# A four-layer graph network on one Trainium2 core: the second hop and the first node stage joined slot by slot, three addition tables cleared in the setup, list work spread between other slots

## The chip, the cores and the metric

One core of a Trainium2 chip. The metric is the device time of the whole program in microseconds (us), lower is better. One launch computes everything.

## The reference, cut to what matters

50000 nodes with 256 features (f32), 50000 edges sorted by destination. Four layers, each `x = layernorm(x + layer(x))`:

```python
# layer 0: two hops of a normalised graph convolution
for _ in range(2):
    msg = segment_sum(norm[:, None] * h[src], dst, N)
    h = 0.5 * msg + 0.5 * x
h = relu(h) @ W.T + b
# layers 1, 2: attention over incoming edges (8 heads), with edge features
attn = softmax over the edges of one dst of leaky_relu(scores)
out  = segment_sum(h_src * attn, dst) + bias
# layer 3: filtered messages, summed by SOURCE node, then two dense layers and a batch norm
msg = x[dst] * (silu(rbf @ Wf1 + bf1) @ Wf2 + bf2)
agg = segment_sum(msg, src, N)
h = silu(agg @ Wu1 + bu1) @ Wu2 + bu2; out = x + batchnorm(h)
```

## The kernel before, in words

Rows (edges or nodes) are padded to 50176 = 128 partitions x C = 392 columns; partition p holds the rows p*392 to p*392+391. Nodes are kept in "edge order": a node's row stands where its first or last edge stands, and nodes without an edge stand at free places. Lists made in the setup say which node's input (`input_i`), which turn of rows (`turn_i`) and which final row (`node_i`) belongs to each place. A stage runs over slots of G = 2 or 4 columns, with a ring of NS buffers per tile. Each engine has its own program; `hold` waits on the semaphore of an earlier slot or stage. The number beside a stage in `unrolled`/`written` is its lag in slots. A stage ends, and so does every `nc.Block()`, only when all five engines, SyncE (SP) among them, have come to its end. SP and ScalarE issue plain DMAs, GpSimd (POOL) the indirect ones: gathers by a list and adding scatters.

The stages, in order, with the first line of each one's main gather where it has one:

- `setup` (L155 to L640). Block 1: 28 loads and 5 small fills from SP (L211, L214), then one DMA of all of x into the table XT (L215, 50176 rows of 1 KB), while VectorE (DVE) prepares flags. Block 2: a histogram of degrees and in-counts, one column at a time (L344, L345 DVE, L354 POOL, L363 ScalarE, L372 and L375 TensorE), with a ring of 4. Block 3: short arithmetic. Block 4, nearly all DVE: `locate` and `compress` (L498 to L524) for two lists, FREE and EMPTY, a join over TensorE, `expand` (L538 to L556) for EMPTY, then SP writes four numbers per node into XT (`XT<-degs`, L637, 50176 runs of 32 bytes); meanwhile DVE runs `expand` for FREE and makes `input_i`; two gathers of border rows `brow` (L630, L631) wait for the write and feed `turn_i`.
- `hop_edges(0)` (gather L681 from XT) and `hop_edges(1)` (gather L681 from S0): slots of 2 columns, ring of 7. Hop 1 per slot: 2 gathers of S0 rows, a load of XE rows (L660), DVE mixes them (L733) and adds along the destination's run (L742), SP stores the sums to the table S1 (L669). A small block at the end carries the last run of each partition over to the place `start_e`.
- `layer_nodes(0)` (gather L879 from x by `input_i`): slots of 2 columns, ring of 4. Load of S1 rows (`st`, L863), 2 gathers of x, DVE mixes (`yt`, L925), adds the bias (L894), adds the product (`z`, L946), and runs the layer norm's statistics; ScalarE rectifies and copies; TensorE transposes, multiplies by W0, transposes, multiplies by the next layer's table weights; ScalarE stores X1 and T1.
- `attention_edges(1)`, `layer_nodes(1)`, `attention_edges(2)`, `layer_nodes(2)`: the attention stages have slots of 4 columns and a ring of 4. SP's order there is, per step: edge attributes of slot t (L1095), store of S of slot t-2 (L1101), then `empty`: a 512 KB DMA of zeros into the addition table A[layer-1] (L1105).
- `filter_edges`: slots of 2 columns; the first column of a slot is added into A[0], the second into A[1] by an adding scatter (L1386); each waits until the one before it on the same table has landed. DVE's compare (L1467) and ScalarE's copy wait for the adds of four slots earlier.
- `update_nodes`: loads A[0] and A[1], adds them (DVE), two dense layers (TensorE), stores. `finish_nodes`: batch norm, layer norm, gather L1635, output.

Of the kernel before, what the change touches and what calls it, by code (L numbers as in the profile page):

```python
# [18 lines left out]
P = 128  # L19
D = 256  # L20
H = 8
# [61 lines left out]
def build(nc, N, x, src, dst, dst_prev, dst_next, ew, rbfT, attr3T, attr64T, w0T, b0, w1T, w1, a1, encW, bias1,  # L83
# [33 lines left out]
    def dram(name, rows, width):  # L117
        return nc.dram_tensor(name, (rows, width), F32).ap()
# [8 lines left out]
    A = [dram("A0", NP + P, D), dram("A1", NP + P, D)]  # L127
    HT = nc.dram_tensor("HT", (P, K, C * P), F32).ap()

    with ExitStack() as keep:  # L130
# [5 lines left out]
        isfirst, notfirst, islast, notlast, follows = [sb(n, [P, C]) for n in ("isfirst", "notfirst", "islast", "notlast", "follows")]  # L136
        head_i, tail_i, start_e = sb("head_i", [P, 1], I32), sb("tail_i", [P, 1], I32), sb("start_e", [P, 1], I32)
# [15 lines left out]
        stats = sb("stats", [P, K, C // 2, 6])  # L153


        def setup():
            with ExitStack() as ctx:
# [3 lines left out]
                def sem(name):  # L161
                    return semaphore(name)

                dst_f, prev_i, next_i, near = tmp("dst_f", [P, C]), tmp("prev_i", [P, C], I32), tmp("next_i", [P, C], I32), tmp("near", [P, C])
# [7 lines left out]
                rowid, free, empty, frees, empties = [tmp(n, [P, C]) for n in ("rowid", "free", "empty", "frees", "empties")]  # L172
                firsts, lasts = tmp("firsts", [P, C]), tmp("lasts", [P, C])
                below = tmp("below", [P, 2])
                deg, ok, dinv, sq = tmp("deg", [P, C]), tmp("ok", [P, C]), tmp("dinv", [P, C]), tmp("sq", [P, C])
# [17 lines left out]
                loaded, zeroed, iotas, prep, tr, folds, filled, widened, placed = [sem(n) for n in (  # L193
                    "loaded", "zeroed", "iotas", "prep", "tr", "folds", "filled", "widened", "placed")]
# [12 lines left out]
                with nc.Block() as block:  # L207
                    @block.sync
                    def _(e):
                        for to, frm in loads:  # L210
                            e.dma_start(to, frm).then_inc(loaded, 16)  # L211
                        e.wait_ge(zeroed, 1)
                        for to, frm in fills:
                            e.dma_start(to, frm).then_inc(filled, 16)  # L214
                        e.dma_start(XT[:, 0:D], x.rearrange("p c d -> (p c) d")).then_inc(widened, 16)  # L215

                    @block.gpsimd
                    def _(e):
                        e.memset(zero[:], 0.0).then_inc(zeroed, 1)
                        e.memset(degs[:], 0.0).then_inc(iotas, 1)  # L220
# [20 lines left out]
                    def _(e):  # L241
# [58 lines left out]

                        for node, at, to_i, to, off in ((dst_f, col, part_i, part, over),):
# [11 lines left out]
                    def _(e):  # L313
# [12 lines left out]
                        mm.then_inc(folds, 1)  # L326

                with nc.Block() as block:  # L330
                    NS = 4
                    R = C // NS
                    hots, taken, masks, maskcs = [stage_of(n, NS) for n in ("hots", "taken", "masks", "maskcs")]
# [6 lines left out]
                    def _(e):  # L340
                        def one_hot(i, s):
                            c = bass.ds(i * NS + s, 1)
# [38 lines left out]
                with nc.Block() as block:  # L381

                    clamped, rooted, based, carried = sem("clamped"), sem("rooted"), sem("based"), sem("carried")
                    DEG, NUMBER, LEAD, ROW = 3, 9, 18, 27

                    @block.vector
                    def _(e):
# [17 lines left out]
                        link(e.tensor_tensor_scan(frees[:], unit[:], notfirst[:], 0.0, ALU.mult, ALU.add))  # L405
# [6 lines left out]
                        link(e.tensor_copy(below[:], psB[:, 3:5]))  # L412
# [36 lines left out]
                        link(e.tensor_scalar(m_half[:], m_half[:], 0.5, None, ALU.mult))  # L449

                    @block.tensor
                    def _(e):
                        e.wait_ge(clamped, NUMBER)
                        e.matmul(psB[:, 0:1], before[:], number[:, C - 1:C], start=True, stop=True)
                        e.matmul(psB[:, 3:4], before[:], empties[:, C - 1:C], start=True, stop=True)
                        e.matmul(psB[:, 4:5], before[:], frees[:, C - 1:C], start=True, stop=True).then_inc(based, 1)
# [12 lines left out]
                with nc.Block() as block:  # L469
                    banks.close()  # L470
                    BITS, CODE = 10, 512.0
                    rem, rev, bit, near2 = tmp("rem", [P, C]), tmp("rev", [P, C]), tmp("bit", [P, C]), tmp("near2", [P, P])
                    rowsC, pos, pcol1 = tmp("rowsC", [P, P]), tmp("pos", [P, W]), tmp("pcol1", [P, 1])
                    pk0, pk1, ck0 = [[tmp(f"{n}{j}", [P, 1]) for j in range(2)] for n in ("pk0", "pk1", "ck0")]
                    oh = [[tmp(f"oh{j}{h}", [P, P]) for h in range(2)] for j in range(2)]
                    ohT = [[tmp(f"ohT{j}{h}", [P, P]) for h in range(2)] for j in range(2)]
                    listed, owner = [tmp(f"listed{j}", [P, W]) for j in range(2)], tmp("owner", [P, W])
                    codes, other, moved = [tmp(n, [P, 2, W]) for n in ("codes", "other", "moved")]
                    joint, there, shift = tmp("joint", [P, 2, C]), tmp("there", [P, W]), tmp("lshift", [P, W])
                    ids, r1, r2 = tmp("ids", [P, C]), tmp("r1", [P, C]), tmp("r2", [P, C])  # L480
                    brow = tmp("brow", [P, 2, XW])
                    bank = lambda n: ctx.enter_context(psum(n, [P, 512], F32))
                    psO, psJ, psL = bank("psO"), [bank(f"psJ{j}") for j in range(2)], [[bank(f"psL{j}{h}") for h in range(2)] for j in range(2)]
                    counted, located, turned, ready, assembled, copied, fetched, taken, tabled, placed, bounded = [sem(n) for n in (
                        "counted", "located", "oturned", "ready", "assembled", "jcopied", "lfetched", "ltaken", "rtabled", "placed", "bounded")]
                    EMPTY, FREE = 0, 1

                    @block.vector
                    def _(e):
# [6 lines left out]

                        def locate(j):
                            link(e.tensor_scalar(near2[:], rowsC[:], below[:, j:j + 1], None, ALU.is_le))  # L498
                            link(e.tensor_reduce(pk1[j][:], near2[:], AX, ALU.add))
                            link(e.tensor_scalar(pk0[j][:], pk1[j][:], -1.0, None, ALU.add))  # L500
# [1255 lines left out]
```

## Time and profile before

| | us |
|---|---|
| median of 3 runs | 7849.68 (7843.85 to 7850.1) |
| the profiled execution | 7853.95 |
| its span (first to last instruction) | 7852.0 |
| DVE / PE / POOL / ACT busy in the span | 6030.9 / 4153.3 / 3600.6 / 3581.2 |

PE is TensorE, ACT ScalarE. The profile shows one execution. The rows further down give times from the start of the span. "Busy" leaves out semaphore, register and DMA-issuing instructions; rows with SPq show how long SP was occupied with issuing a DMA.

### The profile page before, as it was taken

What the parts mean: (1) busy time and instruction counts of PE and PEld (TensorE: products, weight loads), DVE (VectorE), ACT (ScalarE), POOL (GpSimd) and SP (SyncE); (2) the same over time, 40 slices, a digit from 0 to 9 for tenths busy, and PEclk for the clock granted to TensorE, in tenths of its full rate; (3) what the DMA queues carried; (4) which work ended last, traced back from release to release, by engine and by line L of the source; (5) the groups of instructions that cost most, each with busy time, mean ns of one, the idle gap of its engine ahead of it and who ended that gap; (6) DMA issues with size and microseconds to landing.
All of it is one profiled execution on the core that took longest, in us unless ns stands there. A gap on an engine that the chain in (4) does not pass through costs nothing. (4 is left out here: it accounts for less than half of the span.)

```text
span 7852.0 us, 84021 instructions
## 1 busy us (share of the span) xinstructions
PE 4153.3 (53%) x18168; PEld 3161.6 (40%) x18168; DVE 6030.9 (77%) x18094; ACT 3581.2 (46%) x9619; POOL 3600.6 (46%) x3559
## 2 busy tenths in 40 slices
PE   7910000039999333335886222000498998999644
PEld 4500000038888222223554222000266666888522
DVE  7896657767776899998998777899888885554676
ACT  4505750038888333334775000234444443444688
POOL 7806767764443333334555555000266662000477
PEclk9955555569999555557998555555699999999755
DMA  9028989978787566667998888677677776666799
GB/s 285 1 6 236 313 295 298 299 252 243 243 243 227 201 220 220 217 219 249 341 342 276 263 264 264 223 251 252 174 114 115 114 113 147 203 203 204 242 316 304
DMA packets 1120799, 1765.08 MB, mean 225 GB/s; under 512 B 227356, under 2 KB 586372, under 8 KB 1120170
## 3 DMA queue, kind: packets, MB, share of 16 engines
q1 hardware_dynamic: 683786, 1019.20, 40.7%
q0 software_dynamic: 188768, 422.51, 21.9%
q10 hardware_dynamic: 247744, 318.00, 11.7%
q8 instruction: 155, 2.54, 0.1%
q14 instruction: 346, 2.83, 0.1%
HBM read 969.63 MB, written 840.95 MB: 231 GB/s over the span
## 5 line engine op out<-in xcount | busy, mean ns | idle before, releaser
L1125 POOL DMA_INDIRECT rows<-T,index_i x784 | 759.4, 969 | 884.2 <-DVE sums L1267 698.5
L817 ACT ACTIVATE xo<-z,shift,rsd 128x256 f32<-128x256 f32 x1568 | 849.8, 593 | 0.4 <-issue 0.2
L1635 POOL DMA_INDIRECT xt<-X,node_i x392 | 370.8, 946 | 908.4 <-POOLq L1702 784.6
L1386 POOL DMA_INDIRECT A<-comb,ai x392 | 617.6, 1575 | 340.4 <-DMA A<-comb,ai 227.1
L1142 PE MATMUL psE<-encs,attr 4*128 4x256 f32 x784 | 369.7, 649 | 635.5 <-DMA attr<-in_attr3T 633.3
L879 POOL DMA_INDIRECT xt<-in_x,input_i x392 | 375.2, 957 | 470.6 <-DVE xb L894 394.2
L766 PE MATMUL psC<-sums,chainT 128*128 128x256 f32 x4 | 2.4, 700 | 1100.6 <-PEq L655 1100.6
L1401 PE MATMUL psH<-rbf,wf1s 20*128 20x256 f32 x784 | 228.4, 411 | 644.7 <-DMA rbf<-in_rbfT 644.7
L789 DVE BATCH_NORM_STATS2 row_stats<-z 128x6 f32<-128x256 f32 x1568 | 564.5, 402 | 0.1
L1142 PEld LDWEIGHTS psE<-encs,attr 4*128 4x128 f32 x784 | 243.9, 326 | 760.9 <-DMA attr<-in_attr3T 702.2
L801 ACT ACTIVATE sd<-mean_var,epsc 128x2 f32<-128x2 f32 x784 | 237.9, 303 | 584.8 <-DVE mean_var L796 583.0
L879 POOL DMA_INDIRECT xt<-X,turn_i x392 | 370.4, 945 | 251.8 <-DVE xb L894 185.0
L1044 PE MATMUL psV<-w2s,xT 128*128 128x272 f32 x1568 | 407.2, 403 | 114.6 <-ACT tt L980 114.6
L681 POOL DMA_INDIRECT rows<-S,index_i x392 | 396.8, 1012 | 122.7 <-issue 99.8
L766 PEld LDWEIGHTS psC<-sums,chainT 128*128 128x128 f32 x4 | 1.0, 310 | 1102.4 <-issue 1102.4
L1142 PE MATMUL psE<-fes,attr 64*128 64x8 f32 x784 | 183.3, 360 | 493.2 <-DMA attr<-in_attr64T 485.2
L681 POOL DMA_INDIRECT rows<-XT,src_i x392 | 379.1, 967 | 141.7 <-issue 100.9
L959 ACT ACTIVATE yt<-yt,m_half 128x256 f32<-128x256 f32 x392 | 183.2, 532 | 559.9 <-DVE yt L925 559.9
L1589 DVE COPY aT<-psA 128x512 f32<-128x512 f32 x196 | 135.5, 691 | 379.1 <-PE psA L1540 379.1
L1401 PEld LDWEIGHTS psH<-rbf,wf1s 20*128 20x128 f32 x784 | 133.8, 189 | 723.9 <-DMA rbf<-in_rbfT 644.8
L742 DVE SCALAR_TENSOR_TENSOR sums<-sums,follows,rows 128x256 f32<-128x256 f32 x784 | 381.1, 486 | 21.3 <-issue 0.3
L1159 ACT ACTIVATE rowsd<-rowsd,isfirst 128x280 f32<-128x280 f32 x392 | 174.9, 516 | 486.0 <-DMA rowsd<-T 486.0
(358 smaller groups left out, 14805.5 us busy)
## 6 DMA issues: line engine op xcount, KB each, us to landing
X<-xo ACTq DMA_DIRECT2D x588, 256.0 KB, 3.6
S<-sums SPq DMA_DIRECT2D x196, 544.0 KB, 2.8
st<-S SPq DMA_DIRECT2D x392, 272.0 KB, 4.2
S<-sums SPq DMA_DIRECT2D x392, 256.0 KB, 4.0
A<-zero SPq DMA_DIRECT2D x196, 512.0 KB
T<-tt ACTq DMA_DIRECT2D x196, 280.0 KB
rowsd<-T SPq DMA_DIRECT2D x98, 560.0 KB
T<-tt ACTq DMA_DIRECT2D x196, 272.0 KB
```

The source lines that it names most:

```text
L681: e.indirect_dma_start(rows[s][:, k, :], None, table, bass.IndirectOffsetOnAxis(ap=at_i[:, c:c + 1], axis=0))\
L742: ins = e.scalar_tensor_tensor(sums[s][:, k, :], last, follows[:, bass.ds(C - (i * NS + s + 1) * G + k, 1)], rows[s][:, k, 0:D], ALU.mult, ...
L789: ins = e.bn_stats(row_stats[s][:, k, :], z[s][:, k, :])
L801: e.activation(sd[s][:, :, 0], mean_var[s][:, :, 1], ACT.Sqrt, bias=epsc[:]).then_inc(signal(rooted, s), 1)
L817: ins = e.activation(y[s][:, k, :], z[s][:, k, :], ACT.Identity, bias=shift[s][:, k, :], scale=rsd[s][:, k, :])
L879: e.indirect_dma_start(xt[s][:, k, :], None, xin, bass.IndirectOffsetOnAxis(ap=at_i[:, c:c + 1], axis=0))\
L1044: mm = e.matmul(psV[k][:, 0:DW], xT[s][:, k, m * P:(m + 1) * P], weights[:, m, :], start=m == 0, stop=m == K - 1)
L1125: e.indirect_dma_start(rows[s][:, k, :], None, table, bass.IndirectOffsetOnAxis(ap=at_i[:, c:c + 1], axis=0))\
L1142: mm = e.matmul(psE[s % 2][:, k * EW:(k + 1) * EW], attr[s][:, k, :], weights[:], start=True, stop=True)
L1386: e.indirect_dma_start(A[k], bass.IndirectOffsetOnAxis(ap=ai[s][:, k, :], axis=0), comb[s][:, k, :], None, compute_op=ALU.add).then_inc(si ...
L1401: mm = e.matmul(psH[s % 2][:, m * G * P:(m + 1) * G * P], wf1s[:, m * P:(m + 1) * P], rbf[s][:].rearrange("p g q -> p (g q)"), start=True, ...
L1635: e.indirect_dma_start(xt[s][:, k, :], None, X3, bass.IndirectOffsetOnAxis(ap=node_i[:, c:c + 1], axis=0))\
```

## The change

1. `hop_edges(1)` and `layer_nodes(0)` become one stage, `hop_nodes`, of 196 slots of 2 columns. The sums go from the hop's DVE add straight to the node part's mix, one slot later, from on-chip memory; S1 is still stored but no longer loaded. A longer block at the end redoes the one row per partition that needs the carry: through both products and the norm, into X1 and T1.
2. `A` has three tables. All are cleared in the setup's block 1 by SP, 294 DMAs of 512 KB; `empty` is gone from the attention stages. The adds of `filter_edges` go round the three tables; `update_nodes` loads and adds a third.
3. List work: the FREE list's `locate`, `distance`, bit and shift steps run one piece per 17 columns inside the histogram; its `shift_right` steps and the making of `input_i` and `turn_i` run one piece per 8 slots in hop 0, where the two `brow` gathers now stand ahead of the first gather. Three small reductions (`fix_sum`, `fix_half`, `fix_i`) are added to block 3.

```diff
+    A = [dram(f"A{t}", NP + P, D) for t in range(3)]
 ...setup, block 1, SP...
+                        e.wait_ge(zeroed, 2)
                         for to, frm in fills:
                             e.dma_start(to, frm).then_inc(filled, 16)
                         e.dma_start(XT[:, 0:D], x.rearrange("p c d -> (p c) d")).then_inc(widened, 16)
+                        for t in A:
+                            for c in range(0, C, QZ):      # QZ = 4
+                                e.dma_start(nodes(t)[:, c:c + QZ, :], wide_zero[:]...).then_inc(emptied, 16)
 ...histogram, DVE...
+                        def one_hot(i, s):
+                            if (i * NS + s) % EVERY == EVERY - 1:      # EVERY = 17
+                                list_free((i * NS + s) // EVERY)
 ...block 4, SP...
                         e.dma_start(nodes(XT)[:, :, D:XW], degs[:]).then_inc(placed, 16)
                         e.wait_ge(placed, 16)
+                        e.wait_ge(emptied, 16 * len(A) * (C // QZ))
 ...hop 0, DVE...
+        unrolled(R, NS, ... [(weigh, 0), (square, 0), (weight, 0), (add, 2), (list_rows, 0)])
 ...hop_nodes (new): POOL, DVE, PE...
+                        every([(gather, 0), (take, 0)])            # 2 gathers of S0, 2 of x
+                        every([(mix_hop, 0), (mix, MIX), (add_hop, 0), (add_bias, MIX), (add, ADD), (ln_invert, APPLY),
+                               (ln_stats, ADD), (ln_shift, APPLY), (ln_measure, ADD)])
+                        every([(turn_r, TURN), (multiply, PRODUCT), (turn_x, TURNX), (tabulate, TABLE)])
+                MIX, TURN, PRODUCT, ADD = 1, 2, 3, 4
+                APPLY, TURNX, TABLE = 5, 6, 7
 ...attention, SP...
-                        written(N, NS, ... [(stage, 0), (store, 2), (empty, 2)])
+                        written(N, NS, ... [(stage, 0), (store, 2)])
 ...filter, POOL...
+                                q = (i * NS + s) * G + k
+                                hold(e, *landed(q - len(A)))
+                                e.indirect_dma_start(A[q % len(A)], ..., compute_op=ALU.add).then_inc(added[q % len(A)], 16)
 ...update, DVE...
+                            e.tensor_tensor(more[s][:], more[s][:], third[s][:], ALU.add)...
```

In `hop_nodes` the rings of the gathers, loads and sums hold 7 slots, the others 4. `gather(t)` waits for the hop's add of slot t-7, `take(t)` (the gather of x) for the mix and bias of slot t-7.

## Rows read from the trace of the kernel before

**Rows 1.** Windows, one per stage; the heading is the first line.

```profile
core 0: us, PE busy (x) PEld busy (x) DVE busy (x) ACT busy (x) POOL busy (x), PEclk, DMA share, GB/s
628.00:1148.00 520.00, 1.19 (x2) 0.50 (x2) 305.43 (x1381) 363.38 (x980) 381.19 (x394) 0.50 0.91 301
1148.00:1680.00 532.00, 1.19 (x2) 0.50 (x2) 367.73 (x793) 0.00 (x0) 398.86 (x394) 0.50 0.88 291
1680.00:2565.00 885.00, 871.86 (x4696) 748.82 (x4696) 614.00 (x1964) 727.46 (x2151) 375.21 (x392) 0.99 0.78 238
...
3600.00:4265.00 665.00, 515.50 (x2369) 370.32 (x2368) 627.23 (x2369) 481.99 (x1570) 374.22 (x396) 0.97 0.98 323
4265.00:4950.00 685.00, 185.21 (x792) 175.76 (x792) 496.11 (x1386) 36.70 (x196) 373.95 (x391) 0.50 0.80 256
...
5595.00:6575.00 980.00, 860.97 (x3532) 602.72 (x3532) 791.65 (x2560) 437.97 (x1184) 618.52 (x393) 0.95 0.69 113
6575.00:7340.00 765.00, 763.97 (x3910) 673.05 (x3911) 379.91 (x779) 327.39 (x781) 0.00 (x0) 1.00 0.63 200
```

**Rows 2.** Timeline, one add in layer_nodes(0): start, us, engine, and idle time before it.

```profile
2100.87 0.69 DVE L946 TENSOR_TENSOR z<-psZ,xb 128x512 f32<-128x512 f32 x1 [1.31 <-issue]
```

**Rows 3.** Groups by line in hop 1: busy us, mean ns, idle before and releaser.

```profile
L681 POOL DMA_INDIRECT rows<-S,index_i x392 | 396.8, 1012 | 122.7 <-issue 99.8 <-DVE sums L742 19.5 <-PEq L655 3.4
L742 DVE SCALAR_TENSOR_TENSOR sums<-sums,follows,rows 128x256 f32<-128x256 f32 x392 | 190.2, 485 | 14.0
L733 DVE SCALAR_TENSOR_TENSOR rows<-rows,w_from,xe 128x256 f32<-128x256 f32 x392 | 173.5, 483 | 139.5 <-DMA rows<-S,index_i 132.0 <-issue 4.4 <-DVE sums L742 0.4
```

**Rows 4.** Timeline of the setup: SP's issues, the histogram's start, the last write, hop 0.

```profile
0.80 0.40 SPq L211 DMA_DIRECT2D src_i<-in_src  x1
...
14.12 0.43 SPq L211 DMA_DIRECT2D bts<-in_beta  x1
...
17.06 0.63 SPq L215 DMA_DIRECT2D XT<-in_x  x1
18.03 0.36 DVE L251 CAST src_f<-src_i 128x392 f32<-128x392 int32 x1 [18.03 <-DMA bts<-in_beta]
...
51.04 1.28 ACT L363 ACT_TABLE_LOAD   x1 [51.04 <-PEq L207]
...
563.46 0.61 SPq L637 DMA_DIRECT2D XT<-degs  x1
...
602.40 1.87 POOL L630 DMA_INDIRECT brow<-XT,dst_i  x1 [227.69 <-SPq L469]
...
628.74 0.94 POOL L681 DMA_INDIRECT rows<-XT,src_i  x1 [22.57 <-PEq L655]
```

**Rows 5.** Timeline of the setup's DVE: begin and end of the FREE list's compress.

```profile
415.23 0.57 DVE L507 TENSOR_TENSOR rem<-cols,frees 128x392 f32<-128x392 f32 x1
...
458.21 0.57 DVE L527 TENSOR_SCALAR owner<-listed 128x784 f32<-128x784 f32 x1
```

**Rows 6.** Windows: the copy of x beside the histogram; a store of S alone.

```profile
100.00:150.00 50.00, 50.00 (x184) 27.54 (x183) 43.08 (x123) 31.47 (x61) 48.27 (x62) 1.00 1.08 320
...
3001.40:3002.70 1.30, 0.00 (x0) 0.00 (x0) 1.19 (x4) 0.88 (x4) 0.99 (x2) 0.50 0.99 378
```

**Rows 7.** Attention 2: SP's issue of the attributes, and PE that waits for them.

```profile
4602.87 0.98 SPq L1095 DMA_DIRECT2D attr<-in_attr64T  x1
...
4607.91 1.87 PE L1142 MATMUL psE<-fes,attr 64*128 64x8 f32 x8 [5.09 <-DMA attr<-in_attr64T]
```

**Rows 8.** Waits in attention 2, 4300 to 4920 us: total, times, longest.

```profile
DVE dot L1237 <- PE psE L1142: 134.8, 85, 3.0
```

**Rows 9.** Waits in attention 1, 2600 to 3560 us.

```profile
DVE enc L1231 <- ACT psX L1165: 24.8, 60, 1.0
```

**Rows 10.** Waits in filter_edges, 5650 to 6500 us.

```profile
POOL A L1386 <- DMA A<-comb,ai: 209.9, 173, 2.1
DVE eq L1467 <- DMA A<-comb,ai: 89.0, 120, 3.0
```

More of the change, by code:

```diff
@@ L326, in _ @@
                         mm.then_inc(folds, 1)
+                        e.wait_ge(freed, 1)
+                        e.matmul(psB[:, 4:5], before[:], frees[:, C - 1:C], start=True, stop=True)
                 with nc.Block() as block:
@@ L574, in _ @@
                         expand(EMPTY, 1)
+                        for b in reversed(range(BITS)):
+                            shift_right(e, link, b)
+                        identify(e, link, ids)
                         link(e.tensor_tensor(ids[:], ids[:], empty[:], ALU.mult))
@@ L682, in gather @@
                                     .then_inc(signal(gathered, s), 16)
+                        if not hop:
+                            for j, c in enumerate((0, C - 1)):
+                                e.indirect_dma_start(brow[:, j, :], None, XT, bass.IndirectOffsetOnAxis(ap=dst_i[:, c:c + 1], axis=0)).then_inc(bounded, 16)
                         unrolled(R, NS, [(gather, 0)])
@@ L1444, in copy @@
                             hold(e, *done(joined, i, s))
-                            hold(e, *done(added[0], i, s, NS))
-                            hold(e, *done(added[1], i, s, NS))
+                            for k in range(G):
+                                hold(e, *landed((i * NS + s - NS) * G + k))
                             e.copy(comb[s][:].rearrange("p g d -> p (g d)"), psM[s % 2][:]).then_inc(signal(copied, s), 1)
@@ L1461, in compare @@
                             hold(e, *done(joined, i, s, NS))
-                            hold(e, *done(added[0], i, s, NS))
-                            hold(e, *done(added[1], i, s, NS))
+                            for k in range(G):
+                                hold(e, *landed((i * NS + s - NS) * G + k))
                             for k in range(G):
@@ L1583, in add @@
                             hold(e, *done(loaded, i, s))
+                            e.tensor_tensor(more[s][:], more[s][:], third[s][:], ALU.add).then_inc(signal(paired, s), 1)
+                            hold(e, *done(paired, i, s))
                             e.tensor_tensor(agg[s][:], agg[s][:], more[s][:], ALU.add).then_inc(signal(summed, s), 1)
```

502 lines of the change are left out of this document (398 added, 104 removed).

## The prediction

> **What bounds the kernel now.** I read the stage windows first [rows 1], then for each touched stage the groups, the waits and a stretch of the timeline. The windows show a sequence of stages with different limits. Hop 1 (532 us) runs no TensorE to speak of and is bound by POOL: its 392 gathers took 396.8 us and the gaps between them 122.7, together 519.5 of 532, or 1.325 us per gather [rows 3]; DVE waits 132 us for the gathers. Layer_nodes(0) (885 us) is bound by PE: busy 871.9 us at a granted clock of 0.99, the 2.4 GHz level; DVE idles 1.31 us before each add [rows 2]. So one stage leaves PE idle and the next leaves POOL (375 of 885 us) and DVE (614 of 885) half idle. The setup is one long DVE chain after the histogram, which starts at 51.0 us when every engine has left block 1 [rows 4]. Attention 2 waits for edge attributes: PE sat 5.09 us before a matmul for a DMA that SP had issued 5.04 us before [rows 7], and DVE waited for that PE 134.8 us [rows 8]. The filter stage waits for its own scatters to land [rows 10].
>
> All sums are made against the profiled execution: span 7852.0, time 7853.95, which is 4.3 us above the median 7849.68. Such a kernel's runs spread by under 0.1%, and 0.2% is about what can be told from no change.
>
> **The fused stage.** It removes the load of S1 and one stage boundary; each slot of 2 columns now has all the rest. Per slot:
> - POOL: 4 gathers. At hop 1's 1.325 us [rows 3]: 5.30. Layer_nodes(0)'s gathers were shorter, 375.2/392 = 0.957 us [rows 1], and with hop 1's gap of 0.31 they would give 5.08.
> - DVE: node part 614.0/196 = 3.13 [rows 1]; hop part 2 x 0.485 + 2 x 0.483 = 1.94 [rows 3]; sum 5.07. Its waits in both stages were for others, and go.
> - PE: 885/196 = 4.52 with the ends, unchanged work. It is no longer the bound.
> - DMA: 4 transfers of 262 KB (S0 rows, XE, S1 store, x rows), X1's 262 KB and T1's 287 KB: 1.60 MB. Layer_nodes(1) moved 323 GB/s at a share of 0.98 [rows 1], so 4.94 us.
> Three resources stand within 7% of each other. The rings of 7 slots give POOL and SP six slots of lead, so I take the longest, 5.30, and not a sum. The ends of the range are 5.07 (DVE alone) and 5.9: the DMA shares of the two stages added, 0.88 x 532/196 + 0.78 x 885/196 = 2.39 + 3.52 = 5.91, as if nothing else overlapped better.
> The stage: 196 x 5.30 = 1039. To it come the first gather's fill (8, an estimate from hop 0, whose first DVE work came 4 us after its first gather and here needs four), the drain of 8 slots (35, an estimate: seven more node slots at about 4.5), and the new end block, some 20 dependent steps with three DMA landings (25, an estimate at 0.5 us a step and 4 us a landing). About 1107 us for the 532 + 885 = 1417, which includes the boundary: **-310**. Range by the slot's two ends: -355 to -193.
>
> **The clock.** PE's share falls from 0.99 to about 4.45/5.3 = 0.84. Layer_nodes(1) held 0.97 with PE busy 515 of 665 us (77%) and the filter 0.95 with 88% [rows 1], so I cost it at nothing. If it fell to the 1.2 GHz level the PE slot would be about 8.9 us (below).
>
> **Clearing three tables in the setup.** 294 DMAs of 524 KB, 154.1 MB, issued by SP in block 1 behind the copy of x. Two prices.
> First, SP's issuing: from src_i to bts 28 loads took (14.12 - 0.80)/27 = 0.49 us each [rows 4]; 294 x 0.49 = 144 us. Block 2 can't start until SP is through, and SP reaches the first clear at 17.7. The copy of x was issued in 0.63 us although it moves 50176 rows, so its descriptors are made after SP has let go; how long the next issue waits is not shown. `XT<-degs`, as many runs, was wholly landed 38.9 us after its issue (563.46 to 602.40) [rows 4], so I take 39. Block 1 then ends at 17.7 + 39 + 144 = 201 instead of 51: **+150**.
> Second, the data. In order behind the copy (51.4 MB at 320 GB/s, to about 180 us [rows 6]), the clears take 154.1 MB at 378 GB/s, the rate of a store of S [rows 6], 408 us, and end near 590. At the copy's 320 they end at 662. The write of degs, at 680 below, comes behind both, so this costs nothing if SP need not wait for the data. Whether it must is what I am least sure of. SP ran ahead of its loads by several microseconds (the last, issued at 14.12, was followed by DVE's start on it at 18.03, with no issue stretched) [rows 4]; but that is some 2 MB, not 154.
> The Trainium skill, "Perfetto Trace Analysis", section "DMA Instruction — HWDGE (DVE, Sync)", says the descriptor generator is locked for one DMA until all its descriptors are made, and that a full buffer makes the DMA engines start before. By that rule SP's clears would advance no faster than the data, once the buffer is full; the 0.63 us row contradicts it for the issuing instruction itself and leaves it open for the next. It is the first rival below.
>
> **List work.** FREE's locate and compress leave block 4: 458.2 - 415.2 = 43 [rows 5] and about 3 of small steps. In the histogram DVE was busy 43.1 of 50 us [rows 6], so it has 0.138 x 326 = 45 us to spare for 46; pieces of 2.5 us meet a ring of 4 columns of 0.83 us, so I take 8 us of stalls. Bounds: 0 and 46. The three reductions add 4. `degs` is then ready at 563.5 + 150 + 8 + 4 - 46 = 680. The write's landing is next late: 39, to 719; FREE's expand before it is some 12 us and hidden, and the rest, the shifts, input_i and turn_i (about 50 us), moves to hop 0. There DVE is busy 305 of 520 us [rows 1] and a piece of 4 us meets a ring of 7 slots of 2.6 us: nothing, 50 if the cover failed. The two brow gathers, 1.9 us each [rows 4], now stand before hop 0's first. Hop 0's first gather: 719 + 1.5 + 3.7 = 724 against 628.7 [rows 4]: the setup costs **+95** in all (+50 if the copy holds up nobody, +210 if SP resumes only when the copy has ended near 180).
>
> **Attention 2 and 1.** Without the 512 KB of zeros the attribute DMA is issued half a microsecond earlier and lands behind 0.55 MB instead of 1.07. At 378 GB/s that is 1.4 us earlier [rows 6], 1.9 in all, against DVE's wait of 134.8/85 = 1.6 us per slot [rows 8]. **-130**; bounds 0 and -150. The next limit is DVE itself. Attention 1's DVE waited 24.8 us [rows 9] and was else busy: **-5**, bounds 0 and -25.
>
> **Filter.** With three tables a scatter waits for the third before it. POOL's 209.9 us and DVE's 89.0 us in 850 [rows 10] both end on landings. DVE gets back at most 89.0 x 980/850 = 103, then it is the bound (busy 792 of 980 plus gaps), PE close behind: **-90**, bounds 0 and -110. Update: a third load and a DVE add of about 0.7 us per slot; PE is busy 764 of 765 and DVE 380, DMA 0.63 [rows 1]: **+8**, bounds 0 and +30.
>
> **Sum.** -310 + 95 - 130 - 5 - 90 + 8 = -432; 7854 - 432 = **7422**, the median 4 lower: **7418**. Its own range is 7310 to 7560.
>
> **Rivals.**
> A. SP is held at the pace of the data. Then block 1 ends at about 588 instead of 201, and the setup costs 95 + 387 = 482: 7854 - 527 + 482 = **7809**. For it: 22 times more data in wait than the trace shows anywhere. Against: no stretched issue in that trace. A variant, a queue that holds a third of the clears, gives some 7640.
> B. The same hold, with the clears at the copy's 320 GB/s instead of 378: block 1 ends near 660, the setup costs 554, **7881**, slower than before. It decides from the point where block 1 lasts beyond about 650 us, that is, clears below 330 GB/s. For it: the copy beside the same histogram; against: it both reads and writes memory, with 1 KB rows.
> C. PE's clock falls in the fused stage. Slot 8.9, stage 1810 instead of 1107: **8125**, slower. The rows that stand at 0.50 are stretches in which PE was busy under 30% of the time [rows 1].
> D. The three near-equal resources hinder each other, slot 5.9: +118, **7540**. I count it within my own range.
>
> **How the numbers follow.** My forecast with D 0.62, A's variant 0.10, A 0.18, B 0.07, C 0.03. The time is that of the first. The range 7300 to 7810 leaves out half of A's upper side, B, C and a fused slot or filter better than its bound. Faster by over 0.2%: 0.87 (all but B, C and a few of A that come close); same 0.03; slower 0.10.
>
> **What would show it.** Right: the histogram begins near 200 us, hop 0 near 724, the clears' data ends before degs is written; the fused stage has gathers back to back at about 1.3 us, PE's clock above 0.9 and a slot of 5.3; attention 2 near 555 us with no wait on psE; the filter near 890 with POOL waiting little. Wrong: SP's clear issues stretched to about 1.4 us each and the histogram's start near 590 (A); a clock of 0.5 in the fused stage (C); attention 2 unchanged (the attributes were late for another reason).

## The result: 1.5% faster, a quarter of what was forecast

The changed kernel took 7735.6 us (median of 4 runs, 7727.0 to 7740.7), the kernel before 7849.9 on the same chip: ratio 0.9855, 95% interval 0.9837 to 0.9872. The forecast was 7418. What happened is rival A, whose sum was 7809.

The windows of the changed kernel, one per stage (columns as in [rows 1]):

```profile
0.00:553.00 553.00, 5.30 (x24) 4.79 (x24) 27.01 (x59) 0.00 (x0) 6.21 (x19) 1.00 1.03 376
553.00:1076.00 523.00, 350.13 (x1220) 189.44 (x1220) 455.44 (x1059) 206.58 (x396) 308.04 (x392) 0.84 0.13 8
1076.00:1612.00 536.00, 1.19 (x2) 0.50 (x2) 356.17 (x1428) 357.56 (x980) 397.25 (x395) 0.50 0.88 292
1612.00:2692.00 1080.00, 948.45 (x4718) 755.01 (x4718) 945.85 (x2764) 735.93 (x2163) 786.71 (x789) 0.98 0.88 292
...
4362.00:4966.00 604.00, 190.79 (x816) 180.78 (x816) 502.32 (x1394) 38.89 (x199) 379.24 (x393) 0.50 0.65 206
...
5601.00:6411.00 810.00, 790.98 (x3528) 595.87 (x3528) 751.14 (x2548) 435.07 (x1177) 616.16 (x393) 0.98 0.81 133
6411.00:7227.00 816.00, 782.00 (x3920) 665.88 (x3920) 531.10 (x978) 329.20 (x784) 0.00 (x0) 0.99 0.78 252
```

The first row answers the question. For 553 us DVE works 27, PE 5, POOL 6, and the DMA engines are full (share 1.03). Nothing computes while the tables are cleared. Its timeline (start, us, engine) and the row of line 301, the clears (ns min/median/max, first and last start):

```profile
17.77 0.63 SPq L298 DMA_DIRECT2D XT<-in_x  x1
18.44 158.66 SPq L301 DMA_DIRECT2D A<-wide_zero  x1
553.73 1.28 ACT L481 ACT_TABLE_LOAD   x1 [553.73 <-PEq L290]
1081.54 0.94 POOL L737 DMA_INDIRECT rows<-XT,src_i  x1 [0.30 <-issue]
```

```profile
L301 SPq DMA_DIRECT2D A<-wide_zero x294: 432/1248/158661, 18.4 to 552.1; - x147
```

The copy of x is still issued in 0.63 us, but the clear behind it is held for 158.7 us, from 18.4 to 177.1. The other 293 take 1.25 us each at the median: SP moves on at the pace at which the data leaves. The last is issued at 552.1, and the histogram, which began at 51.04 before [rows 4], begins at 553.7. The stretch of the clears alone, and for later the first 305 us of the histogram:

```profile
158.00:553.00 395.00, 0.00 (x0) 0.00 (x0) 0.00 (x0) 0.00 (x0) 0.00 (x0) 1.00 1.03 402
553.00:858.00 305.00, 295.46 (x1052) 159.66 (x1053) 282.33 (x777) 184.04 (x354) 277.21 (x354) 0.99 0.02 8
```

A reader who looks for SP among the waits doesn't find it. The rows to look at are the long issue and the idle time before the other engines' first instruction of the next block, which ends with "PEq".

By stages, between the same first instructions in both traces, against the forecast:

| | before | after | difference | forecast |
|---|---|---|---|---|
| block 1 | 51.0 | 553.7 | +502.7 | +150 |
| rest of the setup | 577.7 | 527.8 | -49.9 | -55 |
| hop 0 | 520.0 | 535.3 | +15 | 0 |
| hop 1 + layer_nodes(0) | 1423.6 | 1077.5 | -346 | -310 |
| attention 1 | 1038.5 | 1012.9 | -26 | -5 |
| attention 2 | 700.4 | 601.5 | -99 | -130 |
| filter | 966.1 | 808.8 | -157 | -90 |
| update | 777.4 | 820.1 | +43 | +8 |

The rest is level; the sum is -116. The setup's +453 ate what the fused stage and the filter gave.

The fused stage's two groups of gathers (busy us, mean ns, idle before), against hop 1's in [rows 3], show POOL's queue with gaps of 0.31 us, as forecast:

```profile
L973 POOL DMA_INDIRECT xt<-in_x,input_i x392 | 393.3, 1003 | 119.5 <-issue 106.7
L966 POOL DMA_INDIRECT rows<-S,index_i x392 | 388.4, 991 | 122.6 <-issue 118.3
```

### The profile page after: what moved, and what is told of

It is laid out like the page before. It is cut to its first block and busy times, and to the rows that moved or that the text cites. A ratio compares the mean times of both kernels' runs of the same rounds, so it can differ in the third digit from the quotient of the medians.

```text
span 7735.7 us, 84360 instructions
## 1 busy us (share of the span) xinstructions
PE 4176.2 (54%) x18180; PEld 3149.3 (41%) x18180; DVE 6105.6 (79%) x18308; ACT 3583.2 (46%) x9626; POOL 3625.7 (47%) x3562
## 5 line engine op out<-in xcount | busy, mean ns | idle before, releaser
L490 PE MATMUL psDeg<-hotc,hot 128*128 128x392 f32 x784 | 326.5, 498 | 514.7 <-DVE hotc L463 514.7
L472 POOL TENSOR_SCALAR mask<-rows,part 128x128 bf16<-128x128 f32 x392 | 308.0, 790 | 575.8 <-POOLq L290 546.8
L973 POOL DMA_INDIRECT xt<-in_x,input_i x392 | 393.3, 1003 | 119.5 <-issue 106.7
L1111 PE MATMUL psV<-w1s,xT 128*128 128x272 f32 x1568 | 405.9, 402 | 68.7 <-ACT tt L1065 63.7
L490 PEld LDWEIGHTS psDeg<-hotc,hot 128*128 128x128 f32 x784 | 139.7, 192 | 606.5 <-DVE hotc L463 540.3
L1097 PE MATMUL psZ<-w0s,rT 128*128 128x256 f32 x1568 | 376.3, 383 | 7.8 <-DVE z L1025 7.2
```

Source lines behind the costliest of these rows:

```text
L490: e.matmul(psDeg[:, 0:C], hot[:, s, :], hotc[:, s, :], start=first and s == 0, stop=last and s == NS - 1)
L973: e.indirect_dma_start(xt[t % NH][:, k, :], None, x.rearrange("p c d -> (p c) d"), bass.IndirectOffsetOnAxis(ap=input_i[:, column(t, k)], ...
L1111: mm = e.matmul(psV[k][:, 0:DW], xT[t % NS][:, k, m * P:(m + 1) * P], w1s[:, m, :], start=m == 0, stop=m == K - 1)
```

## The experiments

They ran on several chips, which fall into two kinds. On the first kind (the result's chip is one of them) the kernel before takes 7844 to 7851 us, on the second 8046 to 8059. Ratios hold within one kind only, and each run below says which it had. All code is cut to what was changed.

### 1. The clears put beside the histogram

```diff
@@ block 1 @@
-  for t in A: for c in range(0, C, QZ): e.dma_start(nodes(t)[...], wide_zero...)
@@ block 2, SP @@
+  clear(e, clears[0:180])
@@ block 3, SP @@
+  clear(e, clears[180:220])
@@ block 4, SP, before the write of degs @@
+  clear(e, clears[220:])
```

> The changed kernel, with the 294 clears issued by the same engine and in the same order, but 180 of them in the block of the histogram, 40 in the block after it and 74 in the listing block ahead of the degree columns' write; none is left in the first block. Theory 1 (the clears cost what they hold the issuing engine back in a block that has little other work, because the block's end waits for that engine): the first block ends near 51 us again, the histogram runs from 51 to about 390, the last clear is issued near 552, the degree columns land some 40 us later, the first gather of hop 0 starts near 600 instead of 1081.5, and the kernel takes 7736 - 481 = 7255 us (7220 to 7300). Rival 1 (the clears cost by their bytes, 154 MB at 402 GB/s = 383 us, wherever they are, because they contend with what they run beside): first gather near 960 to 1080, time 7620 to 7740. Rival 2 (the histogram's block is only as long as the clears in it, so the stall moves one block on): first gather near 740, time about 7395.

First kind: 7267.4 us, ratio 0.9265 (0.9252 to 0.9278), 468 us below the changed kernel, with the same 294 transfers. Theory 1 stands, rivals 1 and 2 fall. The timeline of 'beside':

```profile
53.95 504.57 SPq L294 DMA_DIRECT2D A<-wide_zero  x294
412.01 0.56 DVE L522 TENSOR_SCALAR deg<-psDeg 128x392 f32<-128x392 f32 x1 [20.52 <-PEq L426]
463.42 0.36 DVE L641 COPY pos<-cols 128x392 f32<-128x392 f32 x1 [15.74 <-PEq L503]
571.31 0.60 SPq L701 DMA_DIRECT2D XT<-degs  x1
614.48 0.95 POOL L746 DMA_INDIRECT rows<-XT,src_i  x1 [0.30 <-issue]
```

SP is held for 504 us, nearly as in the changed kernel, but the other engines work beside it. And the clears cost the histogram nothing that can be told. From its first matmul on in-counts to its last it takes 337.3 us in 'beside' and 336.7 in the changed kernel. The last 235 us, in 'beside' with the DMA engines full and then in the changed kernel with no clears beside it:

```profile
158.00:393.00 235.00, 228.71 (x823) 123.27 (x823) 219.05 (x594) 141.96 (x274) 216.84 (x273) 1.00 1.02 395
653.00:888.00 235.00, 228.69 (x824) 123.26 (x823) 220.51 (x598) 141.94 (x274) 218.10 (x275) 1.00 0.00 1
```

The 20.52 us before block 3 (2.88 in the kernel before) and the 15.74 before block 4 are the same fault in small. 180 clears were some 18 us too many for the histogram's block, and 40 were too many for block 3's 36 us of DVE work. That is why the first gather came at 614.5 and not near 600, as expected.

### 2. One clear left in block 1; clears twice as wide

```diff
+  clear(e, clears[:1])      # in block 1; the rest as in 'beside'
```
```diff
-  QZ = 4
+  QZ = 8
```

> The kernel of the run 'beside', but with one of the 294 clears left in the first block, behind the copy of the input into 50176 rows; the others are where they were (179, 40 and 74). Theory 1a (the first transfer behind the copy is held until the copy is nearly through, 140 us, so one clear is enough to hold the block): the first block ends near 160 us instead of 54, the histogram and all behind it come some 106 us later, first gather of hop 0 near 715, time near 7365 us. Theory 1b (only the sum of many clears holds the engine; a single one is taken at once): the first block ends near 54 and the time is that of 'beside', 7267. The 40 clears of the third block also show how far the issuing engine runs ahead of the data once nothing is queued before them: there they are issued at 0.49 us each until it is held again.

> The changed kernel with clears twice as wide: 147 transfers of 1 MB instead of 294 of 512 KB, all in the first block as there. Theory 1 (the issue goes at the pace of the bytes, 402 GB/s): 2.6 us a clear, first block ends near 553 as with 294, time 7736 (7700 to 7760). Rival (1.25 us is what one transfer costs its issuing engine, whatever its size): 158 + 147 x 1.25 = 342, histogram 211 us earlier, time near 7525.

Both fell on the second kind: 7908.9 us (0.9831) and 8245.1 us (1.0238). The setup alone is read, since it takes the same on either kind (in the changed kernel block 1 ends at 553.7 and 554.7, and hop 0 begins at 1081.5 and 1079.5). With one clear the histogram begins at 177.4: a single transfer behind the copy holds the block 124 us longer. Theory 1a stands (the expectation had read the 158.7 us as the hold's end and not as its length, hence 160). In block 3, where nothing was queued any more, SP got three clears away in 1.7 us (517.73 to 519.40) and was then held again, at 1.26 us each (rows of 'one_clear'):

```profile
177.40 1.28 ACT L486 ACT_TABLE_LOAD   x1 [177.40 <-PEq L296]
```

```profile
517.73 2.86 SPq L294 DMA_DIRECT2D A<-wide_zero  x4
519.40 11.33 SPq L294 DMA_DIRECT2D A<-wide_zero  x9
```

With 147 clears of 1 MB the issue takes 2.15 us instead of 1.25, and block 1 ends at 524, not at 342. So the pace goes by the bytes and not by the number of transfers. The wide clears were 30 us quicker in all (421 GB/s in 177 to 521, against 402), which neither theory said.

```profile
L301 SPq DMA_DIRECT2D A<-wide_zero x147: 432/2146/158336, 18.3 to 521.4; - x147
```

So of block 1's 503 us more, 126 are the hold behind the copy (51.0 to 177.1) and 377 the clears' bytes. No run tells what about the copy holds the next issue, its 50176 separate rows or its 51.4 MB: the hold is as long as the data takes (160 us at 322 GB/s), and both would give that.

### 3. The fused stage alone

```diff
-  for phase in (hop_nodes, ...
+  for phase in (lambda: hop_edges(1), lambda: layer_nodes(0), ...
```

> The kernel of the run 'beside' with the fused stage taken out again: second hop and first node stage run as the two stages that they were before, after the same hop 0. Theory 1: the two stages take the 1425 us that they took before, against 1079 fused, so the time is that of 'beside' + 346: about 7600 us. Rival (part of the 346 is the TensorE clock, 0.81 over the two stages before and 0.98 in the fused one, and would have come without fusing): the granted clock of the node stage stays at 0.98 here and the difference is 250 us or less, about 7500.

First kind: 7618.4 us (0.9712; 0.9699 to 0.9725), 'beside' + 351. Hop 1 and the node stage took 1427 us, and the node stage's window has PE at 870 of 885 us and a clock of 0.99, as in [rows 1]. Theory 1 stands and the rival falls. The granted clock of the node stage is 0.99 here, as it was before, and 0.98 in the fused stage, so it adds nothing to the 351 us. The lower average over the two stages comes from hop 1 (0.50), in which PE is busy 1.2 of 532 us.

### 4. Two tables instead of three

```diff
-  A = [dram(f"A{t}", NP + P, D) for t in range(3)]
+  A = [dram(f"A{t}", NP + P, D) for t in range(2)]
   # and 196 clears, and no third load and addition in update_nodes
```

> The kernel of the run 'beside' with two addition tables instead of three: 196 clears, two tables in the filter stage's rotation, two loads and one addition a slot in the update stage. Theory F (the filter stage's 157 us came from the third table): filter stage 967 us again; setup 22 us shorter (last clear near 403, so the degree columns wait for nothing and the first gather is near 578); update stage 42 us shorter; time = 'beside' + 157 - 22 - 42 = + 93, about 7348 us. Rival (the filter's gain came from the rest of its edits, and the tables' number does nothing): filter stage near 810, time = 'beside' - 64, about 7190.

First kind: 7357.7 us (0.9382; 0.9369 to 0.9395), 'beside' + 90 against + 93 expected. Filter 956 us, update 777, setup 17 us shorter. Theory F stands: of the filter's 157 us, 144 are the third table, which costs 39 in the update and 17 in the setup even where the clears are hidden. Waits (total, times, longest) in the filter stage of 'beside_two', then of the changed kernel:

```profile
POOL A L1765 <- DMA A<-comb,ai: 222.4, 173, 2.5
PE psM L1803 <- DVE fl L1877: 79.8, 136, 2.8
DVE eq L1846 <- DMA A<-comb,ai: 89.2, 143, 2.9
```
```profile
POOL A L1756 <- ACT comb L1817: 98.7, 170, 0.8
POOL A L1756 <- DMA A<-comb,ai: 20.4, 67, 0.3
```

### 5. The update stage: two tries at 43 us

```diff
-  unrolled(R, NS, [(add, 0), (copy, 0), (measure, 3)])   # beside_upd, DVE
+  unrolled(R, NS, [(add, 0), (copy, 1), (measure, 3)])
```
```diff
-  unrolled(R, NS, [(load, 0), (store, 4)])               # beside_store6, SP
+  unrolled(R, NS, [(load, 0), (store, 6)])
```

> The kernel of the run 'beside' with one number changed in the update stage: VectorE's copy of the turned rows runs one slot behind its additions (lag 1 instead of 0), so that the two additions of the next slot stand ahead of the copy that waits for TensorE. Theory U1 (the update stage's 42 us are the second addition standing in the chain addition, transpose, copy, which leaves TensorE waiting): update stage 816 to about 780, time = 'beside' - 35. Rival U2 (the third load is the cause: 768 KB a slot at 252 GB/s come too late): update stage unchanged within 5 us. Rival U3 (the copy one slot later holds the hidden product back): stage longer by 10 us or more.

> The kernel of the run 'beside' with one number changed in the update stage: the store of a slot's result stands six slots behind the loads in the issuing engine's order instead of four. Theory U4 (the third load comes late because the engine that issues it stands at the store of four slots back, which waits for the second product: the loads go out some two slots ahead of their use instead of four): VectorE's wait for the third table, 106 us, falls under 40, TensorE's wait for the sum, 45 us, to the first slot's 20, and the stage goes from 817 to about 780: time = 'beside' - 35 = 7232 us. Rival U2 (the transfers themselves, 252 GB/s at 0.78 of the queues' time, are the limit): unchanged within 5 us.

'beside_upd' (first kind): 7272.0 us, 5 above 'beside', stage 823. U1 falls: more slack for DVE doesn't help, since it waits for the third table. (The 6 us more say nothing: with the stage unaltered it took 817, 820 and 822 us in three kernels.) 'beside_store6' (second kind, 7773.0 us, 0.9652): its update stage takes 779.8 us. That stage takes 777 to 779 with two tables on either kind, and 817 to 823 with three and the store at lag 4. U4 stands, U2 falls. The waits of the changed kernel's update, and those of 'beside_store6':

```profile
DVE more L1955 <- DMA third<-A: 109.1, 141, 20.6
PE psA L1911 <- DVE agg L1957: 46.9, 42, 20.9
```
```profile
DVE more L1964 <- DMA third<-A: 20.7, 1, 20.7
PE psA L1920 <- DVE agg L1966: 23.1, 2, 21.0
```

What is left is the first slot. The ring has four slots. By the order of the code SP's loads could go out only some two slots ahead, because the store of four slots back stood before them and waited for the second product. With two loads a slot this sufficed, with three not. With the store at lag 6 the stage's rate rose from 252 to 265 GB/s, so the transfers had not been the limit.

### 6. Hop 0's list work behind the slots

```diff
-  ..., (add, 2), (list_rows, 0)]
+  ..., (add, 2)]
+  for t in range(12): list_rows(t, 7)     # after the last slot
```

> The kernel of the run 'beside' with the list work taken out of hop 0's slots and put behind the last slot, in one piece. Theory L1 (hop 0's 15 us more than before are its 51 us of VectorE work between the slots, which the gathers' rhythm hides but for 15): the slots take 520 us again, the list work some 50 us behind them, hop 0 about 570, time = 'beside' + 35 = 7302 us. Rival (the 15 us are from the two boundary gathers and the later start of the queue, nothing of the list): slots 535 again, time = 'beside' + 50 = 7317.

Second kind: 7831.8 us (0.974). Its gathers in hop 0 span 556.0 us from first to last. On that kind the kernel before has 556.9, and the kernels with the list between the slots 565 to 575 ('best' 566.6). Behind the slots the list work keeps DVE at work from 1179 to 1230. L1 stands, and its rival falls. The whole of hop 0 takes 582 us in the kernel before, 593 in 'best' and 629 here: between the slots the list work costs some 10 us, behind them 46. On the first kind it costs 15 between them (gathers' span 497.4 against 512.4).

### 7. Both finds together, and the same kernels on the second kind of chip

'best' has clears[:188] in block 2, up to 214 in block 3, the rest in block 4, and the store at lag 6. (Block 3 then ends with its own work, at 0.54 us of idle, but block 2 holds DVE for 29 us instead of 21: the write of degs starts 8 us earlier than in 'beside'.)

> The kernel of the run 'beside' with both finds put together: 188 clears in the histogram's block, 26 in the next, 80 in the listing block (in 'beside' the 40 of the middle block held it 15.7 us too long), and the update stage's store six slots behind the loads. By the stage times: 7267 - 12 (the middle block ends with its own work) - 37 (update) = 7218 us on a chip on which the kernel before takes 7844 (ratio 0.920). Rival (the clears left over are then held in the listing block, and the degree columns wait for them): 7230 us, ratio 0.922.

> The changed kernel, unaltered, beside 'best' and the kernel before on one chip: the last four kernels ran on a chip on which the kernel before takes 8046 us instead of 7844, and there hop 0, the fused stage and the last stage were slower by 56, 375 and 93 us than in 'beside'. If this lands on a chip as the first one: 7736 us, ratio 0.986. If on one as the second: by those stages 7736 + 56 + 375 + 93 = 8260 us against 8046, ratio 1.027, slower than before. Rival (those stages were slow by what differs in the kernels): 7736 us wherever the kernel before takes 7844, and a ratio of 0.986 on either.

> The kernel before, unaltered, for its stages' times on the chip of these runs. If the chip is as the second one (8046 us) and it is the gathering stages that are slow there, hop 0 takes some 575 us instead of 520, the last stage 598 instead of 505, and what is left, some 50 us, falls on the second hop and first node stage: 1475 instead of 1425, against 1453 fused. If it is as the first one: the stage times known, 7844 to 7852 us.

All on the second kind: 'best' 7747.8 us, 0.962 (0.9606 to 0.9633); the changed kernel 8268.7, **1.0276** (1.0262 to 1.029), slower than before; the kernel before 8048.6. On the first kind 'stores_sync' below, 'best' but for two stores' queue, took 7226.0, 0.921 (0.9195 to 0.9226), where 'best' was expected at 7218; 'best' itself never ran there. The windows of hop 0, the (joined) stages, attention 1 and the last stage of the kernel before there, then of the changed kernel:

```profile
629.00:1212.00 583.00, 1.19 (x2) 0.50 (x2) 304.53 (x1383) 348.35 (x980) 379.22 (x395) 0.50 0.81 268
1212.00:2682.00 1470.00, 878.13 (x4706) 753.13 (x4706) 981.09 (x2757) 728.88 (x2156) 770.02 (x786) 0.80 0.79 249
2682.00:3721.00 1039.00, 377.19 (x816) 250.02 (x816) 934.22 (x1982) 308.88 (x787) 387.90 (x395) 0.50 0.62 212
...
7451.00:8047.00 596.00, 217.92 (x784) 139.99 (x784) 348.15 (x1378) 429.96 (x982) 370.43 (x392) 0.50 0.80 259
```
```profile
1080.00:1672.00 592.00, 1.19 (x2) 0.50 (x2) 352.42 (x1423) 345.00 (x980) 388.57 (x395) 0.50 0.79 264
1672.00:3112.00 1440.00, 1015.43 (x4718) 831.42 (x4718) 943.87 (x2774) 740.39 (x2163) 780.70 (x793) 0.85 0.68 219
3112.00:4120.00 1008.00, 377.17 (x816) 250.35 (x816) 929.13 (x1973) 308.91 (x787) 383.78 (x391) 0.50 0.50 167
7671.00:8268.00 597.00, 218.44 (x784) 140.37 (x784) 349.09 (x1378) 430.07 (x982) 370.52 (x392) 0.50 0.80 259
```

From the first gather to the next stage's, fusing gives 36 us there (1470.8 to 1435.0) instead of 346. DVE, ACT and POOL are busy as long as on the first kind, the DMA share fell from 0.88 to 0.68: what grew is idle time. Four kernels, all made from 'best', looked for its cause. Three leave work out after the first slots, with the waits for it ('no_xe' the loads of XE, 'no_take' the gathers of x, 'no_tab' three of four matmuls of the last product), so their results are not the reference's; the fourth moves two stores:

```diff
# no_xe: in hop_nodes' load
+  if t >= NH: return
# no_take: in hop_nodes' take
+  if t >= NH: return
# no_tab: in hop_nodes' tabulate
+  if t and (k, m) != (G - 1, K - 1): continue
# stores_sync: store and store_table moved from ScalarE's list to SP's, lags NH + 5 and NH + 7
```

> The kernel of the run 'best' with the fused stage's load of the second-hop rows left out after the first seven slots (the same seven tiles are read again and again, so the sums are not those of the reference): 50 of its 315 MB less. Theory M1 (on the second kind of chip the stage is held by the load on the transfer engines: its idle stretches with nothing to wait for grow with the bytes beside them): fused stage 1441 to 1250 us or less there. Rival M2 (the engines' own instruction streams are late whatever is moved): 1400 to 1441. On a chip of the first kind both give the 1078 us that the gathers' issue allows.

> The kernel of the run 'best' with the fused stage's two stores of results (X1 and T1, 2 of 6 transfers a slot, 105 MB) issued by SyncE instead of ScalarE; bytes and order of the work as they were. Theory M3 (a third queue beside SyncE's and the gathers' is what delays everything on the second kind of chip, and ScalarE, which issues into it, is late with its copies): fused stage 1441 to about 1250 us there. Rival M1 or M2 (the number of queues is nothing): 1441 within 30. On a chip of the first kind: 1078 within 10 either way.

> The kernel of the run 'best' again, as the base for the next two. First kind of chip: 7220 us, ratio 0.920. Second kind: 7748 us, ratio 0.962, fused stage near 1440.

> The kernel of the run 'no_xe' again, for a chip of the second kind: by M1 (load on the transfer engines) fused stage 1250 us or less, by M2 (instruction streams late whatever is moved) 1400 to 1441. First kind: as 'best_b' within 10 us.

> The kernel of the run 'stores_sync' again, for a chip of the second kind: by M3 (a third queue) fused stage about 1250 us, otherwise 1441 within 30. First kind: as 'best_b' within 10 us.

> The kernel of the run 'best' with the fused stage's gathers of the input rows left out after the first seven slots (the first seven slots' rows are used again and again, so the result is not the reference's): 392 + 14 gathers instead of 784. Theory M4 (on the second kind of chip the gathers' path is what is slow, at 1.5 us each in hop 0 and 1.8 in the fused stage): fused stage 1441 to 1050 or less there. Rival M2 (TensorE's instructions come late whatever is moved): 1350 to 1441. First kind: the gathers' issue no longer sets the slot, VectorE with 4.8 us a slot does: 1078 to about 1000.

> The kernel of the run 'best' with three of the four matmuls of each slot's last product left out in the fused stage after the first slot (the table rows are then not the reference's): 588 fewer of 4718 matmuls and about one microsecond of TensorE a slot. Theory M2 (TensorE's instruction stream): fused stage 1441 to 1200 there. Rival M4: 1400 to 1441. First kind: 1078 either way.

'no_xe' (7223.0 us, 0.9207) and 'stores_sync' fell on the first kind, with the fused stage at 1076 and 1078 us, and told nothing of the second. Their repeats, 'no_take' and 'no_tab' ran on the second, whose fused stage, from its first gather to the next stage's, took:

| | us | whole kernel | ratio |
|---|---|---|---|
| best_b | 1434 | 7766.6 | 0.9653 |
| no_xe_b | 1432 | 7756.5 | 0.9637 |
| stores_sync_b | 1425 | 7761.6 | 0.9644 |
| no_tab | 1399 | 7713.3 | 0.9573 |
| no_take | 1008 | 7316.4 | 0.9080 |

```profile
1197.00:2638.00 1441.00, 1024.54 (x4718) 835.53 (x4718) 944.71 (x2776) 741.55 (x2163) 785.03 (x795) 0.84 0.57 185
```
```profile
1198.00:2208.00 1010.00, 929.52 (x4718) 761.42 (x4718) 933.65 (x2765) 731.05 (x2163) 428.47 (x412) 0.96 0.79 262
```

The upper row is 'no_xe_b', the lower 'no_take'. Both leave 50 MB out, one as plain loads, the other as gathers. The first changes nothing, though the rate falls to 185 GB/s. The second takes 426 us off and brings the stage to 4.74 us a slot, where DVE is busy 92%. So M1 and M3 fall, and M2 fails for TensorE's instructions (no_tab gives 35 us of some 200 it should). M4 is right that the number of gathers decides, but not that each gather is slow. POOL's record of one is the same on both kinds, 946 ns at the median, and so is the median from one start to the next in the fused stage, 1.25 us. Their packets take the DMA engines no longer either (26.0% of 1435 us in the changed kernel there, 34.1% of 1077 on the first kind, so 373 and 367 us). The time is lost in pauses: in 'best_b' 51 gathers start more than 3 us after the one before, at most 10.3, which makes some 305 of the 356 us; in 'stores_sync', on the first kind, none does. In a pause POOL waits for DVE, and DVE, before its add of the product, for something that the profile doesn't name. That add in the changed kernel on the first kind (1617 to 2694), then on the second (1672 to 3107):

```profile
L1025 DVE TENSOR_TENSOR z<-psZ,xb 128x512 f32<-128x512 f32 x196 | 133.8, 683 | 4.1 <-issue 4.1
L1025 DVE TENSOR_TENSOR z<-psZ,xb 128x512 f32<-128x512 f32 x196 | 134.6, 687 | 427.6 <-issue 389.1 <-remote 34.2 <-ACT xo L893 4.3
```

What pauses the engines, and why fewer gathers end it, stays open; that the instructions of other engines than TensorE come late is not excluded.

## Why the prediction was wrong

**Failed: "this costs nothing if SP need not wait for the data".** The sum priced the clears at SP's own issue rate, 0.49 us each, read from 28 loads with little in the queue before them. Block 1 was to end at 201 and ended at 553.7. Two terms were wrong. The hold behind the copy was taken as 39 us (from the landing of `XT<-degs`) and is 158.7. The 294 issues were taken as 144 us and are 377, 1.28 us each on average. The prediction saw both and named the doubt ("some 2 MB, not 154"), and then took the price of a short queue for a long one. Runs 'beside', 'one_clear' and 'wide8' show the hold, its two parts and its pace. The trace of before could have settled neither, but the distance by which SP does run ahead, about three clears or 1.6 MB, is of the size that the loads showed there. (By that size the clears were 77 times the data in wait, and not 22 times, as stands beside rival A.)

The Trainium skill, "Perfetto Trace Analysis", section "DMA Instruction — HWDGE (DVE, Sync)", has the descriptor generator locked for one DMA until all its descriptors are made. The next issue's 158.7 us agree with a lock. The copy's own row of 0.63 us doesn't agree with that section of the Trainium skill, in whose timeline a DMA's row lasts until its descriptors are made. That the issues behind it advance at the data's pace is shown by the clears' 1.25 us.

**Rival A** was right in mechanism, with block 1 forecast to end at 588 against 553.7, since the clears ran at 402 GB/s in 158 to 553, faster than a store of S had at 378. That 7735.6 lies inside the stated range of 7300 to 7810 is no merit of the main sum: the range had been drawn to reach into A's side, which had a chance of 0.18. The setup alone was off by 358 us; the other terms' errors add up to only -43: -36 (fused stage), -67 (filter) and -21 (attention 1) against +31 (attention 2), +35 (update) and +15 (hop 0). B's condition (slower clears) did not occur, nor did C's: the clock stayed at 0.98 in the fused stage.

**Right: the fused stage.** POOL sets the slot, 5.21 us (1016.8/195) against 5.30 forecast, with gaps of 0.31 us between gathers; fill, drain and end block came to 56 us against 68. D's mutual hindrance did not show on the first kind of chip. On the second the stage took 1435, longer than D's slot of 5.9 gives.

**The filter's term was too small**, 157 instead of 90. It counted only DVE's own 89 us of waits for landings [rows 10]. But PE waited another 80 us for DVE behind them (row below, same window), and DVE's same 2548 instructions went from 788 to 751 us busy, so DVE was not the bound that the sum set at 792. After, PE is, at 791 of 810 us; its same 3528 matmuls had taken 860 before, at a granted clock of 0.96 against 0.98, and why they got so much shorter no run shows.

```profile
PE psM L1424 <- DVE fl L1498: 80.1, 123, 2.8
```

**Attention 2's was too large**, 99 instead of 130: DVE still waits for TensorE's product of the late attributes.

```profile
DVE dot L1602 <- PE psE L1507: 43.8, 65, 1.5
```

In the kernel before this wait had 142.4 us over the whole stage; the 99 are the difference. **Attention 1's** was too small, 26 instead of 5: DVE's whole wait of 24.8 us [rows 9] is gone.

**The update's +8 became +43.** The bytes and DVE's additions were counted, and the order of SP's queue was not: a third load had to go through a store's wait (experiment 5). **List work**: the rest of the setup came to -50 against -55, with the histogram 13 us longer (323.3 to 336.7) where 8 were forecast; hop 0's was forecast at 0 and cost 15.

**Where the gain went.** The other edits gave 570 us (346 + 99 + 26 + 157 - 43 - 15), and the setup took 453 of them. With the clears beside the histogram the setup is 14 us shorter than before (614.5 against 628.7), and the change is worth 7.4% on this kind of chip.

## What to carry to other kernels

A DMA issue is cheap only while the queue ahead of it is short (0.43 us here, against 1.25 for 512 KB once it was full). A row of large transfers holds its issuing engine for as long as the data takes, and a block's end then holds everyone: put such a row in a block with as much computing as the transfers last, and count what already stands in the queue before it. In a ring, look at the order of the issuing engine's queue and count how many slots ahead the loads really go, not how many buffers there are. And measure a change that raises the rate of gathers on more than one chip: the same kernel was 1.5% faster on one kind and 2.8% slower on another.

## What the runs showed of the hardware that was not expected

- One transfer behind a copy into 50176 rows of 1 KB was held 158 to 160 us at its issue (158.7, 158.1, 158.3 and 160.3 in four traces), about as long as the copy's 51.4 MB take at 322 GB/s (160).
- SP ran ahead of the data by about three transfers of 512 KB ('one_clear', block 3). Clears of 1 MB took 2.15 us each at the median, against 2.50 for two of 512 KB.
- Clears at 395 GB/s beside a histogram that works on chip cost it nothing measurable: 337.3 us against 336.7, PE busy 228.7 of 235 us with and without them.
- Two kinds of chip. In the kernel before, block 1, the attention, filter and update stages agree within 1%; in the changed one attention 2 takes 617 us against 601.5, and the filter 820 against 809. Stages with a gather every 1.3 us differ: hop 0 of the kernel before 520 against 582, its last stage 505 against 596, the fused stage 1078 against 1435. In the fused stage the gathers' rhythm is the same on both (1.25 us at the median), and the difference is pauses of up to 10 us.
